# A transformer decoder layer and a non-local block in float32: reciprocal softmax sums turned on VectorE and spread by DMA instead of on TensorE, and the last perceptron block finished by row tile

## The chip, the cores and the metric

The kernel runs on one core of one Trainium2 chip. The metric is the device time of one execution in microseconds (us). Lower is better.

## What is computed

The reference takes `x` (16 x 256 x 512), a context of the same shape and two masks, all float32. It computes a decoder layer: layer norm, self-attention, layer norm, cross-attention on the context, layer norm, a perceptron of width 2048 with GELU, each with its residual. A non-local block of 1x1 convolutions follows. Cut to what matters here:

```python
def attention(q, k, v, mask):                    # 16 heads of 32 columns
    scores = jnp.einsum('bhqd,bhkd->bhqk', q, k) / jnp.sqrt(jnp.float32(HD))
    scores = scores * mask - 10000.0 * (1.0 - mask)
    probs = jax.nn.softmax(scores, axis=-1)
    return jnp.einsum('bhqk,bhkd->bhqd', probs, v)
...
x = hidden + attention(...) @ w_ao + b_ao        # then the same with the context
mlp_out = gelu(ln_out @ w1 + b1) @ w2 + b2
x = x + mlp_out
...
W = jnp.einsum('bnc,bcm->bnm', theta_x, phi_x) / phi_x.shape[-1]
y = jnp.einsum('bnm,bmc->bnc', W, g_x).transpose(0, 2, 1)
return bn(conv(w_w, w_b, y)) + x
```

## The kernel before

Every matrix product of weights and activations is made of three products of fp32r parts: each operand is split into a high part (ACT) and the rest (DVE), and `product` (L63 to L68) issues high x high, high x low and low x high.

The program has three stages. `step` (16 times) folds the non-local block's phi and g into one 128 x 256 matrix per batch and writes it to DRAM (`m1t`). Then come 16 attention blocks (8 of self-attention, 8 of cross-attention), each of two batches (512 tokens), in 17 bodies `body(r, k)` of 8 slots. Then come 8 perceptron blocks of 16 slots (`m_body`). Bodies 10 to 14 and perceptron blocks 1 to 6 are hardware loops.

A **group** is four heads of one batch; a block has 8 groups, 128 in all. A group goes through the slots of the attention stage as a pipeline, and every engine has its own in-order list of work per slot (`slot` of each engine). Around one group, in the slots that follow each other:

- Slot of its scores: PE `scores` (L850), near the end of a slot.
- Next slot: DVE `mask_scores` (L1361) and `maxima` (L1371). The slot after: ACT `exponential` (L1098), which writes exponentials `p` and row sums `rsum`.
- Slot "own": PE turns the four heads' exponentials (L867, four 128 x 128 transposes for each head, heads 0 and 1 at the slot's start, heads 2 and 3 in its middle). ACT copies them out of PSUM (L1104). DVE takes the reciprocals of the row sums (`inverses`, L1378, a 128 x 8 instruction). POOL copies each reciprocal 32 times side by side (`widen`, L657) into `rwide`. At the slot's end PE weighs the values (`weigh`, L880), unnormalised, into columns 0 to 255 of a PSUM bank, and turns `rwide` with two 128 x 128 transposes (L884) into columns 256 to 511 of the same bank, so that every one of the 32 columns of a head, now partitions, has its head's reciprocals along the tokens.
- Slot after it: ACT copies the turned reciprocals to SBUF (`sums_out`, L1112, tile `rt`), DVE multiplies (`scaled`, L1384), ACT and DVE split the product (`weighed`).

```python
                pe.wait_ge(wide_ok, grp + 1)
                for t in range(TPB):
                    last = pe.transpose(banks[:, bank, S + t * P:S + (t + 1) * P],
                                        rwide[:, t, :, :].rearrange("p j d -> p (j d)"), ident[:, :])
                last.then_inc(done, 1)
```

Between these, PE works on two units of 12 products per slot (q, k, v of the coming block, o of the block before). The o units end in DVE `unit_out` (L1340), which adds a residual tile `res` that SP has loaded (`load_res`, L456) and POOL has added a bias to (`add_bias`, L645); SP stores it (`store`, L460). `res` has two places, so tiles 2 and 3 are loaded when tiles 0 and 1 are stored. POOL also normalises the next block's rows (`normalise`, L640), which PE turns in slots 6 and 7 (`turn_rows`, L776); PE waits there for `ln_x`. POOL begins what it does in a slot only when DVE has the slot's maxima (`until_maxima`).

All DMAs are issued by SP, in order. Within a slot SP waits for whatever a transfer needs before it issues it and all that follow: stores for `y_ok` (late in the slot), loads of rows for `x_lo`, chunks of perceptron weights for the split of an earlier chunk.

At the end of each perceptron block, DVE adds the perceptron's PSUM result to the residual (L1587, four row tiles of 128 x 512, after one semaphore for all four), ACT and DVE split two row tiles at a time (`split_t`, L1246 and L1548, and the fold matrix, L1248 and L1550), PE makes theta (`theta`), ACT and DVE read it out (L1253, L1556), PE makes the last product (`last_product`), DVE adds (L1564), SP stores (L484). For all blocks but the last this lies inside the next block; for the last one it is the tail of the program (`after`), where the two batches' products share two PSUM banks and the two places of `res`.

## Time and profile before

| | |
|---|---|
| median of 3 runs | 2146.6 us (2146.05 to 2148.44) |
| time of the profiled execution | 2146.55 us |
| its span, first to last instruction | 2144.6 us |
| TensorE (PE) busy | 2111.4 us, 98% of the span |
| VectorE (DVE), ScalarE (ACT), GpSimd (POOL) busy | 65%, 56%, 22% |
| granted TensorE clock, mean | 0.996 of full speed |
| DMA | 126.24 MB, mean 59 GB/s |

"Busy" is the union of an engine's instructions in time, so overlapping ones count once. A mean duration of one matmul is longer than its distance to the next, since matmuls are pipelined. "Idle before, releaser" is the time an engine stood still before an instruction and who ended it. The chain is followed back from the last instruction, at each step to what released it.

### The profile page before, as it was taken

How to read it: one execution, taken by the hardware profiler on the slowest of the kernel's cores; microseconds unless marked ns; L12 is line 12 of the kernel's file. 1: busy time of each engine (PE TensorE's matmuls, PEld its weight loads, DVE VectorE, ACT ScalarE, POOL GpSimd, SP SyncE). 2: the span in 40 equal slices, each digit the busy share in tenths (PEclk: the TensorE clock that was granted, in tenths of full speed). 3: DMA queues.
4: the chain of work that ended last, by engine and by line, in shares of the span. 5: the costliest groups of instructions: out<-in, count | busy, mean ns of one | idle time of the engine just before them, and what ended most of it. 6: DMA issues, size and time to landing. Idle time of an engine off the chain costs nothing.

```text
span 2144.6 us, 42719 instructions
## 1 busy us (share of the span) xinstructions
PE 2111.4 (98%) x14690; PEld 1684.0 (79%) x14690; DVE 1396.8 (65%) x3693; ACT 1203.9 (56%) x3396; POOL 465.7 (22%) x515
## 2 busy tenths in 40 slices
PE   8989999999999999999999999999999999999998
PEld 7867777777777777777777776778888888888886
DVE  7687877777778877787877879565343343435333
ACT  4387878777888888787887878521111111111111
POOL 1012021111114233223223221043031230313000
PEclk9999999999999999999999999999999999999999
DMA  8410110110121231122122021321101011101001
GB/s 281 137 46 21 40 60 21 41 60 27 35 99 55 75 105 55 51 74 70 38 68 83 24 79 65 106 85 45 42 22 44 20 44 39 40 24 44 22 23 44
DMA packets 77273, 126.24 MB, mean 59 GB/s; under 512 B 7504, under 2 KB 25040, under 8 KB 77136
## 3 DMA queue, kind: packets, MB, share of 16 engines
q1 hardware_dynamic: 77136, 124.45, 17.4%
q8 instruction: 81, 1.33, 0.3%
q14 instruction: 56, 0.46, 0.1%
HBM read 97.16 MB, written 27.26 MB: 58 GB/s over the span
## 4 chain that ended last, share of the span: by engine, by line
PE 91%; DVE 2%; issue 1%; DMA 0%; ACT 0%; DVEq 0%; ACTq 0%
PE A_banks L66 11%; PE A_banks L68 11%; PE A_banks L67 11%; PE A_tp L867 10%; PE A_banks L880 6%; PE A_sc L66 6%; PE A_sc L68 6%; PE A_sc L67 6%; PE A_tp L67 5%; PE A_tp L66 5%; PE A_tp L68 5%; PE A_sc L850 5%; PE A_banks L884 2%; PE A_tp L776 1%; DVE A_p L1371 1%
## 5 line engine op out<-in xcount | busy, mean ns | idle before, releaser
L1098 ACT ACTIVATE A_p<-A_p,A_nmax 128x256 f32<-128x256 f32 x1024 | 510.7, 510 | 0.0
L1361 DVE TENSOR_TENSOR A_p<-A_sc,A_mk 128x1024 f32<-128x1024 f32 x256 | 312.3, 1220 | 203.8 <-PE A_tp L867 203.8
L1104 ACT ACTIVATE A_pt<-A_tp 128x512 f32<-128x512 f32 x512 | 278.6, 596 | 235.9 <-PE A_tp L867 235.9
L1371 DVE CUSTOM_DVE_ANT_0 A_p<-A_p,A_ma 128x256 f32<-128x256 f32 x1024 | 381.1, 427 | 5.5
L867 PE MATMUL A_tp<-A_ident,A_p 128*128 128x128 f32 x2048 | 266.0, 273 | 1.4 <-ACT A_pt L1104 1.4
L867 PEld LDWEIGHTS A_tp<-A_ident,A_p 128*128 128x128 f32 x2048 | 235.0, 141 | 20.1 <-issue 2.4
L1098 ACT ACTIVATION_READ_ACCUMULATOR A_p<-A_p,A_nmax 128x1 f32 x1024 | 205.4, 201 | 0.0
L657 POOL COPY A_rwide<-A_rinv 128x256 f32<-128x256 f32 x128 | 51.4, 401 | 693.2 <-DVE A_ct_l L1391 693.2
L1231 ACT ACTIVATE A_mk<-A_tp,A_cols 128x512 f32<-128x512 f32 x62 | 42.7, 689 | 276.8 <-PE A_tp L68 276.8
L1231 ACT ACTIVATE A_ma<-A_tp,A_cols 128x512 f32<-128x512 f32 x62 | 42.7, 688 | 247.9 <-PE A_tp L68 247.9
L66 PE MATMUL A_banks<-A_xt_h,A_w_h 128*128 128x512 f32 x384 | 161.9, 421 | 0.0
L68 PE MATMUL A_banks<-A_xt_h,A_w_l 128*128 128x512 f32 x384 | 152.1, 396 | 0.0
L67 PE MATMUL A_banks<-A_xt_l,A_w_h 128*128 128x512 f32 x384 | 151.4, 394 | 0.0
L66 PE MATMUL A_tp<-A_xt_h,A_w_h 128*128 128x512 f32 x368 | 145.7, 396 | 0.0
L67 PE MATMUL A_tp<-A_xt_l,A_w_h 128*128 128x512 f32 x368 | 145.6, 396 | 0.0
L68 PE MATMUL A_tp<-A_xt_h,A_w_l 128*128 128x512 f32 x368 | 145.5, 395 | 0.0
L1533 DVE CAST A_h_h<-A_ma 128x512 fp32r<-128x512 f32 x64 | 31.5, 492 | 172.8 <-ACT A_ma L1231 169.0
L880 PE MATMUL A_banks<-A_pt,A_v 128*32 128x256 f32 x2048 | 139.0, 389 | 0.0
L1533 DVE CAST A_h_h<-A_mk 128x512 fp32r<-128x512 f32 x64 | 35.2, 549 | 158.9 <-ACT A_mk L1231 156.2
L744 POOL TENSOR_TENSOR A_v<-A_v,A_b_row 128x512 f32<-128x512 f32 x32 | 53.7, 1700 | 381.0 <-DMA A_v<-x 381.0
L66 PE MATMUL A_banks<-A_w_h,A_ct_h 128*128 128x512 f32 x256 | 107.5, 420 | 0.0
L67 PE MATMUL A_banks<-A_w_l,A_ct_h 128*128 128x512 f32 x256 | 100.9, 394 | 0.0
(223 smaller groups left out, 5032.3 us busy)
## 6 DMA issues: line engine op xcount, KB each, us to landing
A_x<-x SPq DMA_DIRECT2D x96, 256.0 KB, 3.7
A_res<-x SPq DMA_DIRECT2D x64, 256.0 KB, 2.7
x<-A_res SPq DMA_DIRECT2D x64, 256.0 KB, 2.3
A_e<-ctx SPq DMA_DIRECT2D x16, 512.0 KB, 4.2
A_e<-ctx_t SPq DMA_DIRECT2D x16, 512.0 KB, 6.5
A_e<-L_xattn_w SPq DMA_DIRECT2D x32, 256.0 KB, 3.1
A_v<-x SPq DMA_DIRECT2D x32, 256.0 KB, 2.8
out<-A_res SPq DMA_DIRECT2D x32, 256.0 KB, 2.0
```

What stands on the lines that cost most here:

```text
L66: pe.matmul(out, sh, mh, start=first, stop=False)
L67: pe.matmul(out, sh, ml, start=False, stop=False)
L68: return pe.matmul(out, sl, mh, start=False, stop=last)
L850: last = pe.matmul(sc[:, j, t * S:(t + 1) * S], qp[rr, f, rows_], kp[rr, f, keys], start=(n == 0), stop=(n == 2))
L867: last = pe.transpose(tp[:, j % 2, c * S + t * P:c * S + (t + 1) * P], p[:, g % 2, j, t, c * P:(c + 1) * P], ident[:, :])
L880: pe.matmul(banks[rr, bank, 0:S], v[:, b * TPB + c, f * P + j * HD:f * P + (j + 1) * HD], pt[:, j, c, :], start=(c == 0), stop=(c == TPB - 1))
L1098: act.activation(p[:, g % 2, j, t, :], p[:, g % 2, j, t, :], ACT.Exp, scale=-1.0, bias=nmax[:, g % 2, j, t:t + 1], accum_out=rsum[:, g % 2 ...
L1104: act.activation(pt[:, j, :, :], tp[:, j % 2, :].rearrange("p (c s) -> p c s", c=TPB), ACT.Copy)\
L1231: act.activation(hf[f % 4], hidden_bank(blk, f), ACT.Gelu_apprx_tanh, bias=b1_col[:, f:f + 1])\
L1361: dve.tensor_tensor(p[:, g % 2, heads, :, :].rearrange("p j t s -> p j (t s)"), sc[:, heads, :], m, ALU.mult)\
L1371: dve.tensor_tensor_reduce(out=a_, in0=a_, in1=ma[:, b, t, :], scale=-1.0, scalar=BIG, op0=ALU.add, op1=ALU.min, accum_out=nmax[:, g % 2, ...
L1533: dve.tensor_copy(h_h[:, f % 2, :], hf[f % 4]).then_inc(h_hi, 1)
```

## The change

**Reciprocals.** `rinv` becomes 128 x 32 per parity (zeroed once), of which DVE writes 8 columns (one for each pair of row tile and head). A second DVE instruction turns each 32 x 32 block of it: the four blocks' first 8 rows then hold the reciprocals along the tokens. SP writes these four pieces (8 partitions x 128 B each) to a small DRAM tensor `inverses`, waits for them to land, and reads them back with four DMAs, one for each head, each spread over that head's 32 partitions (32 x 2 x 512 B), straight into `rt`. DVE's `scaled` waits for the weighing and for that landing. `widen`, the two transposes of `weigh` and `sums_out` are gone. SP does this first in each slot with an own group, and the two later `load_res` are moved: tiles 0 and 1 from slot 7 to slot 0 of the next body, tiles 2 and 3 from slot 5 to slot 6.

**End of the perceptron.** For the last block alone, the fold matrices are split one slot before the end (with tiles of their own), PE's last `second` signals each row tile, DVE, ACT and DVE again work by single row tiles, the last products of batch 0 go to the two `tp` banks, and the outputs of batch 1 to two tiles of `x`.

The rest: one early fold of four biases is moved by one slot, `w_s` lives in `rt`, and `b2_row` gets smaller.

```diff
+            def store_inverses(r, h):
+
+                grp, _, g = group(r, h, -1)
+                wait_apart(sp, inv_t, grp + 1, ld_i, (grp - 1) * HPG * DMA)
+                for n in range(P // 32):
+                    sp.dma_start(inv_dram[g % 2][:, n * 32:(n + 1) * 32], turned_inv[n * 32:n * 32 + TPB * HPG, g % 2, :])\
+                        .then_inc(st_i, DMA)
+
+            def load_inverses(r, h):
+
+                grp, _, g = group(r, h, -1)
+                wait_apart(sp, st_i, (grp + 1) * (P // 32) * DMA, cx_ok, grp)
+                for j in range(HPG):
+                    rr = slice(j * HD, (j + 1) * HD)
+                    own = inv_dram[g % 2].rearrange("(t j) s -> j t s", j=HPG)[j:j + 1]
+                    sp.dma_start(rt[rr, :].rearrange("p (t s) -> p t s", t=TPB), own.broadcast_to([HD, TPB, P]))\
+                        .then_inc(ld_i, DMA)
...
             def slot(r, k, h, a_, b_, own, pv):
+                if own:
+                    store_inverses(r, h)
+                    load_inverses(r, h)
+                if h == 0 and k > 1:
+                    for t in range(2):
+                        load_res(k - 1, r - 1, t)
+                if h == (6 if k < NU else 4) and k:
+                    for t in range(2):
+                        load_res(k - 1, r - 1, t + 2)
...
                 if h == (5 if k < NU else 3) and k:
                     for t in range(2):
                         store(k - 1, r - 1, t)
-                        load_res(k - 1, r - 1, t + 2)
...
                             store(k - 1, r - 1, t + 2)
-                            if k < NU:
-                                load_res(k, r, t)
...
-                if own:
-                    widen(r, k, h)
...
-                pe.wait_ge(wide_ok, grp + 1)
-                for t in range(TPB):
-                    last = pe.transpose(banks[:, bank, S + t * P:S + (t + 1) * P],
-                                        rwide[:, t, :, :].rearrange("p j d -> p (j d)"), ident[:, :])
                 last.then_inc(done, 1)
...
-                if leaves:
-                    sums_out(r, h, pv)
...
             def inverses(r, h):
                 grp, _, g = group(r, h, -1)
                 dve.wait_ge(exped, (grp + 1) * HPG * TPB)
-                dve.reciprocal(rinv[:, g % 2, :, :], rsum[:, g % 2, :, :]).then_inc(inv_ok, 1)
+                dve.reciprocal(rinv[:, g % 2, 0:TPB * HPG], rsum[:, g % 2, :, :].rearrange("p t j -> p (t j)"))\
+                    .then_inc(inv_ok, 1)
+                wait_apart(dve, inv_ok, grp + 1, st_i, (grp - 1) * (P // 32) * DMA)
+                dve.transpose(turned_inv[:, g % 2, :], rinv[:, g % 2, :]).then_inc(inv_t, 1)
 
             def scaled(r, h, pv):
                 grp, _, g = group(r, h, -2)
-                dve.wait_ge(rt_ok, grp + 1)
+                dve.wait_ge(done, pv[1])
+                dve.wait_ge(ld_i, (grp + 1) * HPG * DMA)
                 wait(dve, c_lo, grp)
...
             def after(items):
-                split_t(NB - 1, 0, True)
-                split_t(NB - 1, 1, True)
+                for t in range(TT):
+                    dve.wait_ge(a_end, t + 1)
+                    add_perceptron(NB - 1, t)
+                    if t == 2:
+                        split_end(0)
+                        split_end(1)
+                split_end(2)
+                split_end(3)
                 for item in items[:2]:
                     theta_out(item, NB, True)
                 for item in items[2:]:
-                    last_out(item, NB)
+                    last_out(item, NB, True)
```

How this moves instructions is shown at three places. First PE at the end of an attention slot (the weighing of a group, then the turns of the next), before:

```order
L850 MATMUL A_sc<-A_k_l,A_q_h 128x256 x4
L850 MATMUL A_sc<-A_k_h,A_q_l 128x256 x4
L880 MATMUL A_banks<-A_pt,A_v 32x256 x8
L884 MATMUL A_banks<-A_ident,A_rwide 128x128 x2
L867 MATMUL A_tp<-A_ident,A_p 128x128 x8
L66 MATMUL A_banks<-A_xt_h,A_w_h 128x512
```

and now:

```order
L876 MATMUL A_sc<-A_k_l,A_q_h 128x256 x4
L876 MATMUL A_sc<-A_k_h,A_q_l 128x256 x4
L906 MATMUL A_banks<-A_pt,A_v 32x256 x8
L893 MATMUL A_tp<-A_ident,A_p 128x128 x8
L66 MATMUL A_banks<-A_xt_h,A_w_h 128x512
```

The two transposes between the weighing and the next turns are gone; nothing else of PE's attention slots has moved.

Second SP's queue in slots 5 to 7 and slot 0 of an attention body, with what each row waits for (`A_y_ok`: DVE's output tile; `A_st_y0`, `A_st_y1`: the store that frees a place of `res`; `A_inv_t`: the turned reciprocals; `A_st_i`: their stores; `A_cx_ok`: the multiply that frees `rt`), before:

```order
L460 DMA x<-A_res 128x512 [waits A_y_ok]
L456 DMA A_res<-x 128x512 [waits A_st_y0]
L460 DMA x<-A_res 128x512 [waits A_y_ok]
L456 DMA A_res<-x 128x512 [waits A_st_y1]
L460 DMA x<-A_res 128x512 [waits A_y_ok]
L456 DMA A_res<-x 128x512 [waits A_st_y0]
L460 DMA x<-A_res 128x512 [waits A_y_ok]
L456 DMA A_res<-x 128x512 [waits A_st_y1]
L441 DMA A_x<-x 128x512 [waits A_x_lo] x4
```

and now, from the stores of slot 5 to those of slot 7:

```order
L471 DMA x<-A_res 128x512 [waits A_y_ok] x2
L502 DMA inverses<-A_turned_inv 8x32 [waits A_ld_i,A_inv_t]
L502 DMA inverses<-A_turned_inv 8x32 x3
L512 DMA A_rt<-inverses 32x2x128 [waits A_cx_ok,A_st_i]
L512 DMA A_rt<-inverses 32x2x128 x3
L467 DMA A_res<-x 128x512 [waits A_st_y0]
L467 DMA A_res<-x 128x512 [waits A_st_y1]
L502 DMA inverses<-A_turned_inv 8x32 [waits A_ld_i,A_inv_t]
L502 DMA inverses<-A_turned_inv 8x32 x3
L512 DMA A_rt<-inverses 32x2x128 [waits A_cx_ok,A_st_i]
L512 DMA A_rt<-inverses 32x2x128 x3
L471 DMA x<-A_res 128x512 [waits A_y_ok] x2
```

The load of residual tiles 2 and 3 stood right behind the stores of tiles 0 and 1; now four stores, a wait for their landing, and four loads stand ahead of it.

Third DVE at the end of the program, before:

```order
L1587 TENSOR_TENSOR A_v<-A_sc,A_v 128x512 x4
L1548 TENSOR_TENSOR A_t_l<-A_v,A_t_h 128x1024
L1550 TENSOR_TENSOR A_m_l<-A_m,A_m_h 128x256
L1548 TENSOR_TENSOR A_xt_l<-A_v,A_xt_h 128x1024
L1550 TENSOR_TENSOR A_xt_l<-A_x,A_xt_h 128x256
L1556 SCALAR_TENSOR_TENSOR A_thx_l<-A_banks,A_cols,A_thx_h 128x512
L1556 SCALAR_TENSOR_TENSOR A_xt_l<-A_banks,A_cols,A_xt_h 128x512
L1564 SCALAR_TENSOR_TENSOR A_res<-A_banks,A_fix,A_v 128x512 x4
```

and now:

```order
L1603 TENSOR_TENSOR A_v<-A_sc,A_v 128x512 x3
L1598 TENSOR_TENSOR A_t_l<-A_v,A_t_h 128x512 x2
L1603 TENSOR_TENSOR A_v<-A_sc,A_v 128x512
L1598 TENSOR_TENSOR A_xt_l<-A_v,A_xt_h 128x512 x2
L1609 SCALAR_TENSOR_TENSOR A_thx_l<-A_banks,A_cols,A_thx_h 128x512
L1609 SCALAR_TENSOR_TENSOR A_xt_l<-A_banks,A_cols,A_xt_h 128x512
L1618 SCALAR_TENSOR_TENSOR A_res<-A_tp,A_fix,A_v 128x512 x2
L1618 SCALAR_TENSOR_TENSOR A_x<-A_banks,A_fix,A_v 128x512 x2
```

The splits of the fold matrices have left the tail, and the splits of the result go by row tile, two of them ahead of the last add.

## Rows read from the trace of the kernel before

**Rows 1.** The page, busy time, share of the span, instructions: TensorE matmuls

```profile
PE 2111.4 (98%) x14690; PEld 1684.0 (79%) x14690; DVE 1396.8 (65%) x3693; ACT 1203.9 (56%) x3396; POOL 465.7 (22%) x515
```

**Rows 2.** Busy time by stretch: PE, PEld, DVE, ACT, POOL, PEclk, DMA share, GB/s

```profile
300.00:700.00 400.00, 400.00 (x3412) 313.68 (x3405) 315.83 (x978) 322.82 (x982) 78.21 (x104) 1.00 0.16 51
...
2100.00:2145.00 45.00, 34.85 (x142) 26.96 (x140) 16.87 (x24) 6.75 (x10) 2.99 (x2) 0.93 0.15 53
```

**Rows 3.** Waits: engine line, waited for, us in total, times, longest us

```profile
ACT A_pt L1104 <- PE A_tp L867: 235.9, 251, 3.6
DVE A_p L1361 <- PE A_tp L867: 203.8, 122, 3.1
```

**Rows 4.** Timeline of PE where a slot ends: start us, us, engine, line

```profile
603.79 1.07 PE L880 MATMUL A_banks<-A_pt,A_v 128*32 128x256 f32 x16
604.79 0.44 PE L884 MATMUL A_banks<-A_ident,A_rwide 128*128 128x128 f32 x2
605.07 1.04 PE L867 MATMUL A_tp<-A_ident,A_p 128*128 128x128 f32 x8
```

**Rows 5.** Groups of PE: busy us, mean ns of one, idle before

```profile
L884 PE MATMUL A_banks<-A_ident,A_rwide 128*128 128x128 f32 x256 | 56.2, 301 | 0.0
```

**Rows 6.** Instructions on tile rt: duration ns min/median/max, first and last start

```profile
L1112 ACT ACTIVATE A_rt<-A_banks x128: 379/391/396, 126.4 to 1366.8; 128x256 f32<-128x256 f32 x128
```

**Rows 7.** Timeline of DVE, slots 5 and 6 of an attention body

```profile
587.29 0.19 DVE L1378 RECIPROCAL A_rinv<-A_rsum 128x8 f32<-128x8 f32 x1
...
596.90 0.19 DVE L1378 RECIPROCAL A_rinv<-A_rsum 128x8 f32<-128x8 f32 x1
597.01 0.37 DVE L1384 TENSOR_TENSOR A_cx<-A_banks,A_rt 128x256 f32<-128x256 f32 x1
```

**Rows 8.** DMA issues: KB each, median us from issue to landing

```profile
A_x<-x SPq DMA_DIRECT2D x96, 256.0 KB, 3.7
A_res<-x SPq DMA_DIRECT2D x64, 256.0 KB, 2.7
x<-A_res SPq DMA_DIRECT2D x64, 256.0 KB, 2.3
...
out<-A_res SPq DMA_DIRECT2D x32, 256.0 KB, 2.0
```

**Rows 9.** Timeline of SP's queue: time from first to last issue

```profile
617.31 1.85 SPq L441 DMA_DIRECT2D A_x<-x  x4
```

**Rows 10.** Timeline of POOL in slot 6, and of PE in slot 7

```profile
602.05 2.56 POOL L645 TENSOR_TENSOR A_res<-A_res,A_o_bias 128x512 f32<-128x512 f32 x2 [2.33 <-DVE A_nmax L1371]
604.57 1.54 POOL L640 TENSOR_SCALAR A_x<-A_x,A_nmean,A_rstd 128x512 f32<-128x512 f32 x2
...
611.00 1.03 PE L776 MATMUL A_tp<-A_ident,A_x 128*128 128x128 f32 x8
```

**Rows 11.** Timeline of the end of the program

```profile
2126.33 0.39 PE L67 MATMUL A_sc<-A_w_l,A_h_h 128*128 128x512 f32 x1
2126.56 0.39 PE L68 MATMUL A_sc<-A_w_h,A_h_l 128*128 128x512 f32 x1
2126.98 2.48 DVE L1587 TENSOR_TENSOR A_v<-A_sc,A_v 128x512 f32<-128x512 f32 x4 [3.59 <-PE A_sc L68]
2128.30 1.06 ACT L1246 ACTIVATE A_t_h<-A_v 128x1024 fp32r<-128x1024 f32 x1 [6.10 <-DVE A_v L1587]
...
2129.39 1.23 DVE L1548 TENSOR_TENSOR A_t_l<-A_v,A_t_h 128x1024 fp32r<-128x1024 f32 x1
...
2130.72 0.47 PE L66 MATMUL A_banks<-A_t_h,A_thw_h 128*128 128x512 f32 x1 [3.78 <-issue]
...
2132.52 0.69 ACT L1253 ACTIVATE A_thx_h<-A_banks,A_cols 128x512 fp32r<-128x512 f32 x1 [1.60 <-PE A_banks L68]
2132.76 0.63 PE L67 MATMUL A_banks<-A_xt_l,A_thw_h 128*128 128x512 f32 x1
...
2140.58 0.75 DVE L1564 SCALAR_TENSOR_TENSOR A_res<-A_banks,A_fix,A_v 128x512 f32<-128x512 f32 x1 [0.43 <-DMA out<-A_res]
```

More of the change, by code:

```diff
@@ L288, in operands, with unit_bank, y_tile @@
                 return (whole, x[:, 0, 0:S], (xt_h[:, 0:TPB, :], xt_l[:, 0:TPB, :]),
-                        (xt_h[:, TPB, 0:S], xt_l[:, TPB, 0:S]), (xt_h[:, TPB + 1, :], xt_l[:, TPB + 1, :]))
+                        (m1_end_h[:, :], m1_end_l[:, :]), (xt_h[:, TPB, :], xt_l[:, TPB, :]))
             return whole, m1[:, :], (t_h[:, :, :], t_l[:, :, :]), (m1_h[:, :], m1_l[:, 0:S]), (thx_h[:, :], thx_l[:, :])
+        def unit_bank(item, end=False):
+            (kind, n, _), (bank, _) = item
+            return tp[:, n[1], :] if end and kind == "p" and n[0] == 0 else banks[:, bank, :]
+        def y_tile(b, o, end=False):
+            return x[:, TPB + o, :] if end and b == BPB - 1 else y[:, o, :]
         def hidden_bank(blk, f):
@@ L993, in hidden, with second @@
                 last.then_inc(h_done, 1)
-            def second(blk, f, first):
+            def second(blk, f, first, end=False):
                 if first:
@@ L1007, in second @@
                                    (hi, lo), f == 0, f == FT - 1)
-                last.then_inc(a_done, 1)
+                    if end:
+                        last.then_inc(a_end, 1)
+                if not end:
+                    last.then_inc(a_done, 1)
             def theta(item, blk, end=False):
@@ L1012, in theta @@
                 m_occupy((kind, b, rel), bank, blk)
-                pe.wait_ge(t_lo, (blk + rel) * BPB + (b + 1))
+                if not end:
+                    pe.wait_ge(t_lo, (blk + rel) * BPB + (b + 1))
                 pe.wait_ge(m1_lo, 1)
@@ L1016, in theta @@
                 for t in range(TPB):
+                    if end:
+                        pe.wait_ge(t_lo, B - BPB + b * TPB + t + 1)
                     cols_ = slice(t * CI, (t + 1) * CI)
@@ L1025, in last_product @@
                 tb = blk + unit[2]
-                m_occupy(unit, bank, blk)
+                if not (end and b == 0):
+                    m_occupy(unit, bank, blk)
                 pe.wait_ge(m1_lo, tb * BPB + (b + 2))
@@ L1030, in last_product @@
                 cols_ = slice(o * P, (o + 1) * P)
-                product(pe, banks[:, bank, :], (mh[:, cols_], ml[:, cols_]), thx, True, True).then_inc(m_done, 1)
+                product(pe, unit_bank(item, end), (mh[:, cols_], ml[:, cols_]), thx, True, True).then_inc(m_done, 1)
             def m_slot(blk, f, first, last, unit, turns):
@@ L1045, in m_slot @@
                         m_turn(item, blk, False)
-                    second(blk, f, first)
+                    second(blk, f, first, last)
             def after(items):
@@ L1105, in turned_out @@
                     .then_inc(pt_ok, 1)
-            def sums_out(r, h, pv):
-                grp, _, g = group(r, h, -2)
-                bank, count = pv
-                act.wait_ge(done, count)
-                wait(act, cx_ok, grp)
-                act.activation(rt[:, :], banks[:, bank, S:2 * S], ACT.Copy).then_inc(rt_ok, 1)
             def weighed(r, k, h):
@@ L1265, in m_slot @@
                     m_turned(item, blk)
+                if last and f == FT - 2:
+                    split_fold(blk, 0, True)
+                    split_fold(blk, 1, True)
             def after(items):
-                split_t(NB - 1, 0, True)
-                split_t(NB - 1, 1, True)
+                for t in range(TT):
+                    split_end(t)
                 for item in items[:2]:
@@ L1562, in last_out @@
                 dve.wait_ge(m_done, count)
-                dve.wait_ge(st_y[o], (NU * 2 + tb * BPB + b) * DMA)
-                dve.scalar_tensor_tensor(y[:, o, :], banks[:, bank, :], fix[:, o:o + 1], t_sb[:, b * TPB + o, :],
+                if not (end and b == BPB - 1):
+                    dve.wait_ge(st_y[o], (NU * 2 + tb * BPB + b) * DMA)
+                dve.scalar_tensor_tensor(y_tile(b, o, end), unit_bank(item, end), fix[:, o:o + 1], t_sb[:, b * TPB + o, :],
                                          ALU.add, ALU.add).then_inc(y_ok, 1)
@@ L1581, in m_slot @@
                     m_turned(item, blk)
-                if f == FT - 1:
+                if last and f == FT - 2:
+                    split_fold(blk, 0, True)
+                    split_fold(blk, 1, True)
+                if f == FT - 1 and not last:
                     n = blk * FT + f
@@ L1585, in m_slot @@
                     for t in range(TT):
[L1586 to L1587 removed]
+                        add_perceptron(blk, t)
             def after(items):
[L1590 to L1591 removed]
+                for t in range(TT):
+                    dve.wait_ge(a_end, t + 1)
[5 more added lines that the diff above has]
+                split_end(3)
                 for item in items[:2]:
```

96 lines of the change are left out of this document (55 added, 41 removed).

## The prediction

> **What bounds the kernel now.** I began with the page's line of busy times [rows 1]: TensorE is busy 98% of the span, VectorE 65%, ScalarE 56%. Busy time alone doesn't say that TensorE is the limit, so I went to the stretches. From 300 to 700 us, inside the attention stage, TensorE shows 400.00 busy us of 400 at full granted clock (1.00, the 2.4 GHz level), with VectorE at 79% and ScalarE at 81% [rows 2]. Then the waits, to see who waits for whom. ScalarE waits 235.9 us for TensorE's turns in 251 places, VectorE 203.8 us in 122 [rows 3]. Over 128 groups that is 1.8 and 1.6 us per slot in which the two stand idle for TensorE. So the attention stage runs at TensorE's pace, and an instruction taken off TensorE there shortens a slot, as long as nothing else needs more than those 1.6 us. The tail is different: in the last 45 us TensorE is busy for 34.85 only, at a mean granted clock of 0.93 [rows 2]. There a chain of adds, splits, products and stores sets the end.
>
> **The turns on TensorE, removed.** There are 256 in 128 pairs, 56.2 us busy, 301 ns each [rows 5]. The distance between starts is what counts. In the timeline a pair starts at 604.79 and the next group's turns at 605.07, 0.28 us later. Those eight turns of the same shape take 1.04 us in all [rows 4]. If the last lasts about as long as the mean of such a turn (301 ns is the nearest row), their seven distances are (1.04 - 0.30) / 7 = 0.106 us each. The first two starts after the weighing are further apart (0.28 for two steps, so about 0.17 and 0.11). That extra belongs to the step from the weighing's shape to a turn's and will stand in front of the next turns instead. So a pair is worth 2 x 0.11 = 0.22 us, and the sum 128 x 0.22 = 28 us. The upper end is 128 x 0.28 = 36 us, if the extra goes too. The lower end is 14 us, if half is given back because the waits that the next turns stand behind (exponentials done, copies out done) are now taken up one after the other where the pair used to cover them. I take 28: the same kind of waits stand before the other turns of a slot.
>
> The Trainium skill ("TensorE: Matmul & The Clock Gate", Part 4: PE-mode transpose) gives a turn about 275 ns in a kernel's context. By that the sum would be an estimated 256 x 0.275 = 70 us. The timeline speaks against it, since the whole pair takes 0.28 us of TensorE's time.
>
> **ScalarE, VectorE and GpSimd in a slot.** ScalarE loses its copy, 391 ns [rows 6]. It waits for TensorE anyway, so that is worth nothing, and it is a reserve. GpSimd loses the widening; it is no bound at 22% [rows 1]. VectorE gains a turn of 128 x 32 and a wait for its own reciprocal. No row shows a turn on VectorE. The nearest are the reciprocal, 0.19 us, and the multiply of 128 x 256, 0.37 us [rows 7]. I take 0.2 for the turn and 0.1 for the wait, since the multiply now starts 0.11 us after the reciprocal's start, overlapped, and the turn cannot. That 0.3 us (ends 0.2 and 0.5) lies within the 1.6 us of idle time. If that cover were gone, it would cost up to 128 x 0.3 = 38 us. Only at the end of the attention stage, where perceptron weights are split as well, do I expect it to show in two or three slots, under 1 us, about what ScalarE's 0.39 gives back there.
>
> **The way through DRAM.** This is the new long wait. From the turned reciprocals to the multiply of the next slot go four stores, their landing, four loads and their landing. An issue costs SP about 1.85 / 4 = 0.46 us, loads of 256 KB back to back [rows 9]. These are smaller, and I keep the price. A store lands 2.3 us after its issue, a load of `res` 2.7 [rows 8]; the new ones are of 1 KB and of 32 KB each, so the times should be no longer while the queue is empty. Round trip: 0.3 + 3 x 0.46 + 2.3 + 3 x 0.46 + 2.7 = 8.1 us. What is there for it: reciprocals start 9.61 us apart (587.29 and 596.90), and the multiply follows its slot's reciprocal by 0.11 [rows 7]. Less the 0.19 of the reciprocal and the 0.22 that the slot gets shorter, that leaves 9.3 us, and VectorE's 1.6 idle us come on top, 10.9 in all. So 8.1 fits, with 1.2 us to spare before anything waits and 2.8 before TensorE does. The last of `done` comes at the slot's end, so nothing is gained on the other side. The load is also held back by `rt`'s single place, but the multiply that frees it comes right behind the reciprocal, long before the stores land.
>
> **SP's queue.** Its eight new issues are 3.7 us per slot, and SP stands about 6 us in a slot's first half. Behind it: in slot 0 two `res` loads and four row loads (2.8 us), with contexts and a mask in the later bodies. They are wanted a slot or more later, so I cost them at nothing. The burst of slot 0 is also ahead of slot 1's small transfers in the DMA queue. Row loads land in 3.7 us [rows 8], one us over the 2.7 taken, which still fits. The tight one is `res` in slot 6. Reciprocal end 597.09 plus 0.3, stores out and landed at +3.7 (601.1), loads issued until 602.9, the first `res` load landed at 605.6, the second half a microsecond later. GpSimd's two adds (2.56) and two normalisations (1.54) [rows 10] used to begin at 602.05. From 605.6 they end at 609.7. TensorE turns those rows at 611.00 [rows 10], 0.2 earlier in the new slot. 1.1 us are left. I cost it at nothing; it is rival B.
>
> **The tail.** Before: last products start 2126.56, one each 0.23 us [rows 11]. Four adds take 2.48 us (0.62 each), and the first waits for all tiles. The chain then goes by halves of 128 x 1024 (ACT 1.06, DVE 1.23) to the first theta product at 2130.72, on to theta's read-out, and to the last add at 2140.58. From there theta's products run at 0.43 us or more apart for a while (the row at 2132.76 lasts 0.63, not 0.39), which is the clock's lower level after 3.78 us without products.
> Now: tile 0's last product is done 9 x 0.23 = 2.1 us before tile 3's, so adds run at 2124.9, 2125.6 and 2126.3. ScalarE's half-size copies (0.6) follow each. DVE splits tiles 0 and 1 from 2127.0 to 2128.3, adds tile 3 until 2128.9, splits tiles 2 and 3 until 2130.2. Theta of batch 0 can start 2127.7, 3.0 us earlier. That of batch 1 ends at 2131.1; read-out 0.7 and 0.75 gives 2132.6. The products of batch 0 don't wait for the other theta's bank, the outputs of batch 1 don't wait for stores. Four final adds back to back from 2132.6, 0.7 each, end at 2135.4, where the last one ended at 2141.3. That is 5.9 us at full clock. Six to twelve products may run at half clock, up to 12 x 0.2 = 2.4 us back, and four stores within 2.8 us may land later than the usual 2.0 [rows 8]. I take 5 us, ends 3 and 6.
>
> **Sum.** 2146.55 (the profiled execution, within 0.1 us of the median 2146.6, so it stands for it) - 28 - 5 = 2113.5 us. The memset, the moved bias fold and the smaller row cost nothing beside TensorE's 100%.
>
> **Rivals.**
> A, half the gain on TensorE: 14 + 5 = 19 us, 2127.6. For it: no row shows the waits of the turns without the pair in front. Against: TensorE shows no gap anywhere between 300 and 700 us. Chance 0.10.
> B, late `res` in slot 6: the normalised rows are late for the turns of slot 7 in 15 bodies. It decides when the chain above is over 1.1 us longer. At transfers landing in 3.7 instead of 2.3 and 2.7 it is 1.4 + 1.0 + 1.0 = 3.4 us longer: 15 x 2.3 = 34 us back, 2147.5, no change; at half of that lateness, 15 x 0.6 = 9 us, 2122.5. Chance 0.12, half of it for each.
> C, the round trip is longer than 10.9 us and sets the slot: slower. At 3.7 us landing for both and 0.46 an issue it is 0.3 + 1.4 + 3.7 + 1.4 + 3.7 = 10.5, just inside. At one us more, since a store must have landed in DRAM before its read may go, it is 11.5: 0.6 over in some 124 slots, 74 us, or 2146.6 - 33 + 74 = 2188. For it: nothing in the trace shows a write that is read back at once, nor pieces of 128 B. Chance 0.07. The Trainium skill ("DMA: Bandwidth & Descriptors", Specifications) says that transfers under 512 B are made by read-modify-write, which these stores are; no run here shows its price.
> D, each turn gives back all its 301 ns: 77 + 5 = 82 us, 2064.5. This is what the skill's rule above amounts to. Chance 0.01.
> The forecast has 0.70. That the change doesn't do what it says is out: in the order of instructions the pair is gone.
>
> **Numbers.** The forecast's own range is 2104.5 (36 and 6 us) to 2123. With A inside and part of B, the range for 8 in 10 is 2103 to 2133. A measurement of this kernel can tell about 0.2%, 4.3 us, from no change. Faster by more than that: the forecast, A, D and the milder half of B, 0.70 + 0.10 + 0.01 + 0.06 = 0.87. Within: the other half of B, 0.06. Slower: C, 0.07.
>
> **What would show it.** Right: distance from the weighing's start to the next turns about 1.06 us instead of 1.28; reciprocals 9.4 us apart in slots like [rows 7]; TensorE still 100% busy in the attention stage; from issue to landing of the small transfers at most 2.7 us; the first theta product 1.1 us after the perceptron's last product starts, not 4.2; the end of the last add 8.9 us after that start, not 14.8. Wrong: a wait of DVE's multiply for the load of `rt` with more than a few us in all (C); TensorE's turn of rows waiting for GpSimd's normalisation (B); a longer "issue" gap in front of the turns (A).

## The result, and the profile after

The changed kernel took 2137.9 us (median of 6 runs, 2132.3 to 2140.8), the kernel before 2147.2 in the same comparison (6 runs, 2146.1 to 2148.4): a ratio of 0.9954, 95% interval 0.9939 to 0.9969. It is faster by 9.3 us, where 33 were forecast; the forecast of 2113.5 us and its range of 2103 to 2133 both miss. Its runs also lie 8.5 us apart, those of before 2.4. The profiled execution took 2140.8 us with a span of 2138.9, so what is read below is one of the slower ones: 5.7 us less than the span before.

The page's busy times and the stretches, with the columns of [rows 1, 2]:

```profile
PE 2092.2 (98%) x14434; PEld 1657.3 (77%) x14434; DVE 1433.6 (67%) x3823; ACT 1171.5 (55%) x3270; POOL 419.1 (20%) x388
```
```profile
300.00:700.00 400.00, 395.26 (x3334) 306.62 (x3327) 331.58 (x1022) 313.49 (x945) 65.48 (x63) 1.00 0.20 64
700.00:1000.00 300.00, 293.18 (x2501) 225.77 (x2500) 245.56 (x759) 233.41 (x705) 77.86 (x70) 1.00 0.26 81
1000.00:1300.00 300.00, 296.24 (x2492) 229.46 (x2492) 247.75 (x768) 232.99 (x707) 67.88 (x64) 1.00 0.23 75
```

TensorE is no longer busy throughout the attention stage: it stands idle 4.7, 6.8 and 3.8 us in these stretches. The end of an ordinary slot, answering to [rows 4]:

```profile
597.36 1.07 PE L906 MATMUL A_banks<-A_pt,A_v 128*32 128x256 f32 x16
598.37 0.87 PE L893 MATMUL A_tp<-A_ident,A_p 128*128 128x128 f32 x6
```

From the weighing's start to the next turns it is 1.01 us, where it was 1.28. The saving is there in every ordinary slot. From one weighing's start to the next (the same row in each slot) it was 9.61 us, 10.48 where rows are turned too; now 9.40 and 10.27. So 0.21 us per slot are saved, where 0.22 were forecast. Yet the last weighing starts at 1365.28 us, against 1365.37 before. What the ordinary slots gain, others give back. The intervals by slot, in us, computed from those starts:

```
body       slot 2   slot 3   slot 7   (bodies 2 to 5: 9.39, 9.41, 10.29)
7          11.17    10.05    14.94
8          11.65    10.57    10.29
9          10.89    10.95    10.29
10         10.19    10.05    10.54
11         9.39     9.92     10.29
12         10.02    10.07    10.29
13         9.39     9.94     10.29
14         9.59     10.05    10.29
15         11.62    10.05    9.44
```

Slot 7 of body 15 has no rows to turn. Over bodies 7 to 15 slot 2 is 9.4 us too long in all, slot 3 7.0, and slot 7 of body 7 4.7. Now the waits (engine line, waited for, us in total, times, longest us), first of VectorE, then of TensorE:

```profile
DVE A_cx L1422 <- DMA A_rt<-inverses: 18.5, 9, 3.4
```
```profile
PE A_banks L66 <- DVE A_cx L1422: 6.3, 5, 2.0
PE A_banks L66 <- DVE A_k_l L1379: 5.1, 10, 1.3
PE A_tp L802 <- POOL A_x L675: 2.8, 2, 2.1
```

The multiply waits 18.5 us for `rt`'s load, in nine slots: one in each of bodies 7 to 15, in slot 2, for the transfers of slot 1. TensorE waits behind it for its bank, and a slot later for k's read-out, which the late multiply pushed back. Below is SP's queue (start, time from first to last issue), first an ordinary slot of body 6, then body 10 from the inverses of slot 0 to the loads of slot 1, and VectorE's rows at the end of the latter:

```profile
562.81 1.28 SPq L502 DMA_DIRECT2D inverses<-A_turned_inv  x4
565.04 1.73 SPq L512 DMA_DIRECT2D A_rt<-inverses  x4
...
856.82 1.32 SPq L502 DMA_DIRECT2D inverses<-A_turned_inv  x4
859.08 1.73 SPq L512 DMA_DIRECT2D A_rt<-inverses  x4
861.11 1.70 SPq L467 DMA_DIRECT2D A_res<-x  x2
863.11 2.11 SPq L452 DMA_DIRECT2D A_x<-x  x4
865.56 1.10 SPq L458 DMA_DIRECT2D A_e<-ctx_t  x2
866.96 0.37 SPq L463 DMA_DIRECT2D A_mk<-mask_Bx1xSxS_ff  x1
867.54 2.07 SPq L502 DMA_DIRECT2D inverses<-A_turned_inv  x4
874.40 1.73 SPq L512 DMA_DIRECT2D A_rt<-inverses  x4
```
```profile
865.93 0.21 DVE L1415 STREAM_TRANSPOSE A_turned_inv<-A_rinv 128x32 f32<-128x32 f32 x1
...
875.06 0.20 DVE L1412 RECIPROCAL A_rinv<-A_rsum 128x8 f32<-128x8 f32 x1
875.34 0.21 DVE L1415 STREAM_TRANSPOSE A_turned_inv<-A_rinv 128x32 f32<-128x32 f32 x1
877.60 0.42 DVE L1422 TENSOR_TENSOR A_cx<-A_banks,A_rt 128x256 f32<-128x256 f32 x1 [2.04 <-DMA A_rt<-inverses]
```

In an ordinary slot the stores are issued right after the turn and the loads 0.95 us after the last store was issued (564.09 to 565.04): SP waits for the stores' landing there, so stores of 1 KB take no longer than that. From the turn's end to the landing of the loads it is about 5.5 us. In body 10 the turn of slot 1 ends at 866.14, but SP is still issuing slot 0's loads until 867.33. Then the four stores stand behind 2.75 MB of slot 0's loads. The loads can only be issued 4.8 us after the last store (869.61 to 874.40), and the multiply starts 11.5 us after the turn's end, having waited 2.04. The longer the delay, the longer the slot: where the multiply starts 10.50 and 10.54 us after the turn's end (bodies 11 and 13), slot 2 loses nothing, at 10.85 (body 14) 0.2, at 11.28 (body 12) 0.6, at 11.46 (body 10) 0.8, at 12.3 (body 7) 1.8. Body 9 alone falls out of this row: 10.65 and 1.5 lost, and there TensorE waits 1.34 us for VectorE's masking.

The 14.9 us of body 7, slot 7, have another chain. Rows of SP, POOL and PE there:

```profile
670.14 0.43 SPq L447 DMA_DIRECT2D A_wst<-L_xattn_w_q  x1
674.05 0.33 SPq L447 DMA_DIRECT2D A_wst<-L_xattn_w_kv  x1
674.49 1.31 SPq L502 DMA_DIRECT2D inverses<-A_turned_inv  x4
677.33 2.42 SPq L512 DMA_DIRECT2D A_rt<-inverses  x4
679.79 0.90 SPq L467 DMA_DIRECT2D A_res<-x  x2
```
```profile
672.57 1.46 POOL L705 TENSOR_TENSOR A_w_l<-A_wst,A_w_h 128x512 fp32r<-128x512 f32 x1
682.86 2.76 POOL L680 TENSOR_TENSOR A_res<-A_res,A_o_bias 128x512 f32<-128x512 f32 x2 [8.83 <-DVE A_nmax L1405]
685.60 2.20 POOL L675 TENSOR_SCALAR A_x<-A_x,A_nmean,A_rstd 128x512 f32<-128x512 f32 x2
```
```profile
686.51 0.63 PE L802 MATMUL A_tp<-A_ident,A_x 128*128 128x128 f32 x4 [2.08 <-POOL A_x L675]
687.86 1.11 PE L802 MATMUL A_tp<-A_ident,A_x 128*128 128x128 f32 x4 [0.72 <-POOL A_x L675]
```
```profile
684.00:688.00 4.00, 1.20 (x7) 0.56 (x6) 4.00 (x10) 1.26 (x5) 4.00 (x5) 0.95 0.28 98
688.00:691.00 3.00, 3.00 (x10) 2.42 (x10) 1.38 (x4) 1.99 (x8) 2.92 (x3) 0.50 0.00 0
```

SP stands in `load_chunk` until GpSimd has split the chunk before (674.03). Slot 6's inverses and the `res` loads behind them go out 4 us late, then GpSimd's add and its normalisation, and TensorE's turn of rows waits, 2.8 us in all. The slot is 4.7 us too long, not 2.8, in part because TensorE, busy for 1.20 of 4 us, then runs 3 us at a granted clock of 0.50 (the 1.2 GHz level; the last two rows are stretches with the columns of [rows 2]).

The tail, answering to [rows 11]:

```profile
2126.78 0.39 PE L68 MATMUL A_sc<-A_w_h,A_h_l 128*128 128x512 f32 x1
2127.96 0.47 PE L66 MATMUL A_banks<-A_t_h,A_thw_h 128*128 128x512 f32 x1 [0.80 <-DVE A_t_l L1598]
```
```profile
2134.16 1.40 DVE L1618 SCALAR_TENSOR_TENSOR A_x<-A_banks,A_fix,A_v 128x512 f32<-128x512 f32 x2
```
```profile
2095.00:2138.90 43.90, 38.51 (x164) 30.00 (x162) 16.98 (x28) 7.88 (x13) 2.98 (x2) 0.99 0.15 55
```

The first theta product starts 1.18 us after the perceptron's last product, the last add ends (2135.56) 8.8 us after it; 1.1 and 8.9 were forecast. From the last weighing to the end of the span it was 779.2 us and is 773.6. The granted clock of the last 44 us is 0.99, where it was 0.93 in the last 45 [rows 2].

### The profile page after: what moved, and what is told of

Same layout as the page of the kernel before. It is cut to its first block and busy times, and to the rows that moved or that the text cites. A ratio compares the mean times of both kernels' runs of the same rounds, so it can differ in the third digit from the quotient of the medians.

```text
span 2138.9 us, 43342 instructions
## 1 busy us (share of the span) xinstructions
PE 2092.2 (98%) x14434; PEld 1657.3 (77%) x14434; DVE 1433.6 (67%) x3823; ACT 1171.5 (55%) x3270; POOL 419.1 (20%) x388
## 5 line engine op out<-in xcount | busy, mean ns | idle before, releaser
L1405 DVE CUSTOM_DVE_ANT_0 A_p<-A_p,A_ma 128x256 f32<-128x256 f32 x1024 | 387.5, 435 | 6.1 <-DVE A_p L1395 0.5
L893 PEld LDWEIGHTS A_tp<-A_ident,A_p 128*128 128x128 f32 x2048 | 229.9, 141 | 73.3 <-issue 51.0
L893 PE MATMUL A_tp<-A_ident,A_p 128*128 128x128 f32 x2048 | 274.2, 277 | 1.7 <-ACT A_pt L1133 1.4
L680 POOL TENSOR_TENSOR A_res<-A_res,A_o_bias 128x512 f32<-128x512 f32 x64 | 82.5, 1310 | 353.3 <-DVE A_nmax L1405 208.3
L1140 ACT ACTIVATE A_ct_h<-A_cx,A_bias_sum 128x256 fp32r<-128x256 f32 x128 | 65.2, 510 | 88.0 <-DVE A_cx L1422 88.0
```

Of the source, the lines that this page charges most:

```text
L680: pool.tensor_tensor(res[:, t % 2, :], res[:, t % 2, :], o_bias[:, int(k >= NB), :], ALU.add)\
L893: last = pe.transpose(tp[:, j % 2, c * S + t * P:c * S + (t + 1) * P], p[:, g % 2, j, t, c * P:(c + 1) * P], ident[:, :])
L1405: dve.tensor_tensor_reduce(out=a_, in0=a_, in1=ma[:, b, t, :], scale=-1.0, scalar=BIG, op0=ALU.add, op1=ALU.min, accum_out=nmax[:, g % 2, ...
```

## Experiments

Three explanations of the missing time are tried. T1 says that slot 0's loads hold up slot 1's round trip. R1 says that GpSimd's work, moved by the later `res` loads, stretches VectorE's maxima, and R2 that VectorE's added turn and wait cost the time. For R1 there is a row: one of the maxima of 128 x 256 takes 1.16 us beside GpSimd's add, where the others take 0.41:

```profile
601.50 1.16 DVE L1405 CUSTOM_DVE_ANT_0 A_p<-A_p,A_ma 128x256 f32<-128x256 f32 x1
...
602.59 0.41 DVE L1405 CUSTOM_DVE_ANT_0 A_p<-A_p,A_ma 128x256 f32<-128x256 f32 x1
```

**1. The tail alone.** The kernel before, with the change of the perceptron's end and nothing of the attention stage's.

> Before with the change's tail alone (perceptron by row tile, own banks and tiles for the last outputs); the reciprocal sums go over TensorE as before. From the last weighing to the end of the span the changed kernel needs 773.6 us, the kernel before 779.2. All theories: 2147.2 - 5.6 = 2141.5 us. Were the tail's gain due to the attention stage's change, it would stay at 2147.

Measured: 2141.2 us against 2148.2, ratio 0.9971 (0.9960 to 0.9982). The tail's 5 us are real: 7.0 by the medians, 6.5 between the profiled spans. So the whole change in the attention stage, some 28 us by the forecast, brought about 3, and even these are not clear of the noise, since the intervals of this run and of the change overlap.

**2. No round trip.** Left out: the way through DRAM, so VectorE multiplies by numbers that are not the reciprocals.

```
-                if own:
-                    store_inverses(r, h)
-                    load_inverses(r, h)
...
-                dve.wait_ge(ld_i, (grp + 1) * HPG * DMA)
```

> The changed kernel with the eight small transfers per head group left out (turned reciprocals stay where they are, VectorE multiplies by whatever the tile rt holds); VectorE's turn, the moved loads of res and GpSimd's moved work stay. T1 (the gain is given back because the loads of slot 0, issued by SP ahead of slot 1's small transfers, hold up the round trip): all but a few us of the 26 that are missing come back, 2112 to 2116 us. R1 (GpSimd's work, moved by the later res loads, runs beside VectorE's maxima and stretches them) or R2 (VectorE's added turn and wait): the missing time stays, 2132 to 2138 us. T1 in the intervals between weighings: slots 2 and 3 of bodies 7 to 15 at 9.4 us instead of 10 to 11.6.

Measured: 2119.7 us, 0.9871 (0.9856 to 0.9886, against before). 18 us come back; slots 2 and 3 of bodies 7 to 15 are at 9.4, but for 9.86 in body 9's slot 2, and slot 7 of body 7 at 10.29. VectorE's turn is still in this kernel, so R2 can't be the bulk. R1 is not tried by it, against what the expectation says: without the round trip SP issues the `res` loads earlier, GpSimd's work with them, and the maxima are busy for 380.9 us, as in the kernel before (381.1), and not the 387.5 of the change. Runs 3 and 7 bear on R1. The time is 4 to 8 us above the 2112 to 2116 of T1, so something is lost elsewhere too (run 10 finds a part).

**3. The burst spread.** One mask, the contexts and body 7's and 8's chunks leave slot 0.

```
                 if h == 0:
                     if k < NU:
                         load_rows(k + 1, r + 1)
-                    if NB <= k + 1 < NU:
-                        load_context(r + 1)
-                    if NB < k < NU:
-                        load_mask(r, 0)
-                    for n in {7: range(0, 4), 8: range(10, 12)}.get(k, ()):
-                        load_chunk(n)
...
+                if h == 1 and NB < k < NU:
+                    load_mask(r, 0)
+                if h in (1, 2) and NB <= k + 1 < NU:
+                    load_context(r + 1, h - 1)
+                if h == 1:
+                    for n in {7: range(0, 4), 8: range(10, 12)}.get(k, ()):
+                        load_chunk(n)
```

GpSimd's addend of that mask goes from slot 0 to slot 1, behind its two adds.

> The changed kernel with slot 0's burst shortened: context loads behind the inverses of slots 1 and 2, mask and weight chunks behind those of slot 1; res and row loads stay in slot 0. T1: bodies 7 to 15 look like bodies 2 to 6 in slots 2 and 3 (9.4 us each), which gives back 2.4 + 3.4 + 3.0 + 1.5 + 0.5 + 1.3 + 0.5 + 0.8 + 2.9 = 16 us by their intervals between weighings: 2121 to 2124 us; the 14.9 us interval of body 7, slot 7, stays. R1, R2: 2136 to 2140 us.

Measured: 2125.8 us, 0.9897 (0.9882 to 0.9912), 12 us less than the change, with the same number of transfers and the same turn on VectorE. All slots 2 and 3 of bodies 7 to 14 take 9.4 us; body 15, whose perceptron chunks and norm rows are still in slot 0, keeps 11.66 and 9.86. The view of tile rt shows what is left of the wait (what it waited for, us, times):

```profile
  DMA A_rt<-inverses: 4.3, 2
```

The wait was 18.5 us in nine slots and is 4.3 in two. The maxima are still stretched (385.7 us), so R1 can't be the bulk either. Run 2 kept the mask's addend in its place and had the short slots too, so the addend's move is not what shortens them: T1 stands. 2 us of the forecast are missing; body 8's slot 0 takes 11.0 us here.

**4. And body 7's chunks a slot apart.** `(7, 5): range(4, 6), (7, 6): range(6, 8)` in place of four chunks in slot 5.

> As the run before, and body 7's weight chunks 6 and 7 are loaded in slot 6 instead of 5, so that SP does not wait in slot 5 for GpSimd's split. If SP's wait for that split is what makes the 14.9 us interval in slot 7 of body 7 (inverse stores 3.9 us late, res loads behind them, then GpSimd's add and normalisation, then TensorE's turn of rows), another 4 to 5 us: 2116 to 2120 us. If that interval comes from the splits' own work on three engines, no difference to the run before.

Measured: 2122.6 us, 0.9885 (0.9870 to 0.9900). Slot 7 of body 7 is back at 10.29 from 14.49. The saving between the medians is 3.2 us where 4 to 5 were forecast, the time is above the expected 2116 to 2120, and the intervals of the two runs overlap; the profile shows the slot itself. The splits are all still there, so it was SP's wait.

**5. Slot 1's transfers on another queue.** ScalarE issues them; SP's burst stays.

```
                     turned_out(r, h, 1)
+                if own and h == 1:
+                    store_inverses(act, r, h)
...
                     weighed(r, k, h)
                 if own:
+                    if h == 1:
+                        load_inverses(act, r, h)
                     turned_out(r, h, 2)
```

> The changed kernel with the eight small transfers of slot 1, and only these, issued by ScalarE on its own DMA queue; slot 0's burst stays on SP, right ahead of them. Control inside the run: slot 2 in bodies 2 to 6, where no long burst stands ahead, shows what eight issues cost ScalarE (at SP's 0.45 us each 3.6 us against some 2.2 idle: intervals of about 10.8 instead of 9.4; if they are cheap for ScalarE, 9.4). Theory Q (the small transfers stand in one queue behind the burst): bodies 7 to 15 have the same slot 2 as bodies 2 to 6; 2122 to 2126 us if cheap, up to 2150 if 0.45 us each. Theory W (the sixteen DMA engines are simply busy with the burst, whichever queue a transfer is in): bodies 8, 9, 10 stay over 1 us longer than bodies 2 to 6; 2135 to 2140 us even if the issues are cheap.

Measured: 2230.1 us, 1.0381 (1.0367 to 1.0394), slower than any case foreseen. The timeline of ScalarE's queue in slot 1, body 3 and then body 10, says why:

```profile
324.92 1.32 ACTq L418 DMA_DIRECT2D inverses<-A_turned_inv  x4
...
327.36 1.76 ACTq L429 DMA_DIRECT2D A_rt<-inverses  x4
```
```profile
911.53 1.42 ACTq L418 DMA_DIRECT2D inverses<-A_turned_inv  x4
...
918.50 1.76 ACTq L429 DMA_DIRECT2D A_rt<-inverses  x4
920.37 1.09 ACT L1145 ACTIVATE A_pt<-A_tp 128x512 f32<-128x512 f32 x2 [5.46 <-issue]
```

The wait for the stores stands in ScalarE's own order: its next copy can't start before the loads are issued, and slot 1 takes 11.2 to 12.8 us in bodies 2 to 6 and 14.6 to 16.3 in bodies 7 to 15. My expectation had priced the issues (they take 0.33 and 0.44 us each, as on SP) and not this wait. It still tells queue and engines apart. In body 3 the loads follow the last store by 1.1 us, in body 10 by 5.5, with no other transfer in ScalarE's queue. So theory W holds: behind a burst a transfer is late in whichever queue it is. The Trainium skill ("DMA: Bandwidth & Descriptors", Issuing engines are not separate DMA queues) says that transfers from all issuing engines run on the same DMA engines; this trace agrees, with its 5.5 us. Only the part in which SP itself is late (1.4 us in body 10) could be gained by another issuer, and no run here shows that gain.

**6. One load for four heads.** The reciprocals stand by head, then row tile, so a head's 256 values are contiguous in DRAM.

```
+                own = inv_dram[g % 2].rearrange("(j t) s -> j (t s)", j=HPG).unsqueeze(1).to_broadcast([HPG, HD, S])
+                sp.dma_start(rt[:, :], own).then_inc(ld_i, DMA)
```

> The changed kernel with one load of 128 KB for the four heads instead of four of 32 KB (reciprocals kept by head, then row tile, so that a head's 256 values are contiguous). SP issues five transfers per slot instead of eight and the load's issue ends about 0.95 us earlier. T1: where slot 1's load lands late it lands 1 us less late, in slots 2 of bodies 7 to 12, 14, 15, and SP's own queue is shorter by the same in slot 0: 8 to 12 us, 2126 to 2130 us. If the stores and their wait behind the burst are all of it and the loads' issues lie elsewhere: 2135 to 2138 us.

Measured: 2127.6 us (2122.7 to 2131.7), 0.9911 (0.9898 to 0.9925), within T1's interval. The wait for `rt`'s load falls to 8.0 us in 6 slots. Three issues fewer per slot are worth 10 us, though not one of them is long. The load's issue takes 0.54 us instead of 1.73, so every round trip is 1.2 us shorter, and slot 0's burst is issued that much earlier: in body 10 slot 1's stores go out 0.1 us after the turn's end instead of 1.4, and the multiply waits 0.1 us instead of 2.04.

**7. The `res` loads in their old places.**

> The changed kernel with the four res loads of a body back in the places of the kernel before: right behind the stores of slots 5 and 7, so that SP waits there until a store has landed. R1 (the later res loads shift GpSimd's work onto VectorE's maxima, and that costs time): the shift is gone, 2130 to 2134 us. T1: SP is held up about 4 us at the start of slots 6 and 0; slot 6's round trip still fits (5.5 + 4 = 9.5 us), slot 0's burst is issued 4 us later and slot 1's inverses land later by up to as much: 1 to 4 us in each of bodies 7 to 15, 2147 to 2170 us.

Measured: 2136.3 us (2130.1 to 2148.8), 0.9954 (0.9937 to 0.9971), the same as the change. Both expectations miss. GpSimd's work is back in its place, and the maxima are busy for 380.3 us again instead of 387.5, at no gain to be seen. The run changes more than that, so it doesn't show by itself that R1 costs nothing: slot 7 of body 7 takes 10.65 us here instead of 14.94, while slot 2 of body 11 takes 13.47 instead of 9.39, and the multiplies wait 19.7 us for `rt` in 10 slots. But slot 7 of bodies 2 to 5, where the change has stretched maxima and this run has none, takes 10.29 us in both. My price for T1 was wrong as well, as SP's queue at body 10 shows:

```profile
853.77 0.33 SPq L467 DMA_DIRECT2D A_res<-x  x1
854.42 1.31 SPq L502 DMA_DIRECT2D inverses<-A_turned_inv  x4
857.18 3.24 SPq L512 DMA_DIRECT2D A_rt<-inverses  x4
860.73 2.18 SPq L452 DMA_DIRECT2D A_x<-x  x4
```

The burst starts later after slot 0's turn, but it has no `res` in it, 0.5 MB less; the multiply of slot 2 waits 2.17 us here, 2.04 in the change.

**8. The best version:** runs 3, 4 and 6 together, and the last body's first perceptron chunks in slots 1 and 2.

> Spread loads (contexts behind the inverses of slots 1 and 2, mask and chunks behind those of slot 1), body 7's chunks a slot apart, the last body's first four perceptron chunks in slots 1 and 2 instead of 0, and the one load of 128 KB. The run with the first two had 2122.6 us; body 15 still had 2.5 + 0.5 us too much in slots 2 and 3. T1: 2117 to 2120 us. Were body 15's excess not from its burst: 2121 to 2123 us.

Measured: 2120.7 us (2118.4 to 2121.5), 0.9875 (0.9861 to 0.9889), 0.7 us above T1's interval and 0.3 under the other case, so the time alone can't choose between them; body 15's slots can. It beats both kernels, the one before by 27 us. Body 15's slots 2 and 3 are at 9.39 and 9.41, and no multiply waits for `rt`'s load any more. SP's queue in slot 1 of body 10:

```profile
851.28 1.31 SPq L501 DMA_DIRECT2D inverses<-A_turned_inv  x4
853.53 0.54 SPq L509 DMA_DIRECT2D A_rt<-inverses  x1
854.41 0.42 SPq L462 DMA_DIRECT2D A_mk<-mask_Bx1xSxS_ff  x1
855.20 0.40 SPq L457 DMA_DIRECT2D A_e<-ctx_t  x1
```

**9. More burst where there was room.** Four loads of 256 KB into a free tile at the end of slot 0 in bodies 2 to 6.

> The changed kernel with four more loads of 256 KB (weights nobody reads, into a tile that is free then) at the end of slot 0's burst in bodies 2 to 6, whose slots 2 and 3 now take 9.4 us each and whose burst is 1.5 MB. With 2.5 MB they have about the burst of body 7 without its context. T1: their DVE multiply of slot 2 now waits for rt's load, 0.5 to 2 us each, and slot 3 is up to 0.6 us longer: 2140 to 2150 us. If the loss of bodies 7 to 15 comes from something else they do (mask addend, context split, chunk splits), bodies 2 to 6 stay at 9.4: 2137 to 2139 us.

Measured: 2139.9 us (2136.2 to 2144.8), 0.9965 (0.9953 to 0.9977): no difference that can be told from the change, and at the edge between the two cases foreseen. Only body 5 got longer (9.59 and 10.03 in slots 2 and 3), the others stayed at 9.4. Their loads did land later, 9.0 to 9.1 us after the turn's end instead of 6.0 to 8.0, but the multiply isn't wanted before 9.3; in body 5 it was 10.7 instead of 6.4. So 1 MB costs 1 to 4 us of landing and in four bodies of five nothing of time; the limit is sharp. T1 had the landing's direction right and left out the slack. In body 5:

```profile
465.50 1.80 SPq L602 DMA_DIRECT2D A_wst<-L_xattn_w_q  x4
467.41 1.71 SPq L503 DMA_DIRECT2D inverses<-A_turned_inv  x4
473.26 2.61 SPq L513 DMA_DIRECT2D A_rt<-inverses  x4
```

**10. No round trip and no turn.** Left out besides what run 2 leaves out: VectorE's turn of the reciprocals and its wait.

> As the run without the round trip (2119.7 us), and VectorE's turn of the reciprocals and its wait left out as well. There the attention stage saved 20.8 us between first and last weighing where 28 were forecast; bodies 1, 8, 9 and 16, in which VectorE also splits weights, fold biases or splits perceptron chunks, gave 0 to 1.4 us less than 1.66. If VectorE's extra 0.35 us per slot is what they miss: up to 4 bodies x 8 slots x 0.35 = 11 us, of which at most the missing 7 come: 2113 to 2117 us. If they are bound by something that neither has: 2118.5 to 2120.5 us.

Measured: 2116.8 us (2116.3 to 2117.6), 0.9858 (0.9843 to 0.9873), 2.9 less than run 2 by the medians; the intervals of the ratios overlap. The profiled last weighings are 2.3 us apart, 1.3 of it in the last body's five intervals (43.8 us, 45.1 in run 2) and 0.4 each in bodies 9 and 15; body 8 is the same. Body 1 takes 77.5 us for its eight slots (79.0 in run 2), but body 0 ends 1.4 us later here, so that is no gain. VectorE's turn and wait cost some 2 to 3 us, most of it in the last body.

**11. The bias fold back in slots 0 to 3** of the best version.

> The best version so far (spread loads and one load, 2120.7 us) with the fold of the last bias block in body 1 back in slots 0 to 3 instead of 1 to 4. Body 1's slots 0 and 2 take 10.8 and 10.15 us there. If slot 2's excess comes from the fold standing one slot later: back to about 9.6, and 2119.5 to 2120.5 us. If it is put where its weights (loaded in slot 0, now behind the inverses) are not there yet, VectorE waits in slot 0: 2121 to 2124 us.

Measured: 2124.0 us, 0.9895 (0.9879 to 0.9910), 3.3 more than run 8: the second case. VectorE waits 3.8 us once for the weights, which slot 0 now loads behind the inverses, and slot 1 of body 1 takes 12.5 us. So the moved fold belongs to the change.

## Why the prediction was wrong

**TensorE's turns, 28 us.** The price was right: 0.21 to 0.22 us per slot. The count was not. Without any round trip, the time from first weighing to last falls by 20.8 us, not 28 (run 2). An undisturbed body gives 1.7 us; bodies 0 and 1 give 0.4 together, body 8 0.3, bodies 9 and 15 1.1 each, and the last body's five intervals grow by 0.2. VectorE and ScalarE split weights in most of these; that this is why a shorter TensorE gives little there is argued, and run 10 shows a part of it. I had read 300 to 700 us and multiplied by all 128. Rival A had put the loss at 14 us, twice this one, and by another cause, waits in front of the turns.

**VectorE's turn.** 0.21 us, its start 0.28 after the reciprocal's: as put. That it would show "in two or three slots, under 1 us" was too low: 2 to 3 us by run 10.

**The round trip** was put at 8.1 us and takes 5.5 in an ordinary slot. The Trainium skill ("DMA: Bandwidth & Descriptors", Specifications) has transfers under 512 B made by read-modify-write, without a price; in this trace these stores, in pieces of 128 B, have landed 0.95 us after their issue.

**The step that failed** is the one on SP's queue: the loads of slot 0 "are wanted a slot or more later, so I cost them at nothing", and a landing of 3.7 us was "one us over the 2.7 taken, which still fits". I took the median landing of a row load for the delay of a transfer behind the whole burst. In bodies 7 to 15, with contexts, a mask or chunks in it, the loads of slot 1 were issued 7.3 to 9.5 us after the turn's end instead of 2.3 and landed after 10.5 to 12.7. That is over 9.3, at which the multiply is wanted, and in places over the 10.9 at which I had TensorE begin to wait, a limit that held (slot 2 lost nothing at 10.5 and 0.6 us at 11.3). A row of the kernel before had the number for a transfer behind the burst: the contexts, issued behind the row loads, landed after 6.5 us, the moving of their own 512 KB included.

```profile
A_e<-ctx_t SPq DMA_DIRECT2D x16, 512.0 KB, 6.5
```

With it for the landing of the stores, in place of 2.3, my own sum would have given 12.3 us, over the 10.9, in the bodies with a context (an estimate from that row). Between the change and run 2 the profiles' last weighings are 20.9 us apart: 19.6 in bodies 7 to 15, 3.6 up to the end of body 0, less 2.3 in the bodies left. By the medians the two kernels are 18.2 us apart; the change's profiled execution was one of its slower ones. It was rival C's mechanism, but in nine slots and not in 124.

**`res` in slot 6**, rival B: fitted in all bodies but one. In body 7 it failed by 4.7 us, because SP waited for GpSimd's split, which the prediction did not look at. The price of the rival was summed wrong as well: its 3.4 us counts the landing of `rt`'s loads (1.0), for which the `res` loads do not wait, so by its own terms it was 2.4 us longer, 1.3 late and 20 us in 15 bodies, not 34. And the 2123 us that closes the forecast's own range comes from none of the terms' ends.

**The tail.** 5 us forecast, 5.6 by the trace of the changed kernel, 7.0 in run 1 with an interval of about 2.4 us to either side. The sum at full clock was 5.9; of the up to 2.4 us for the lower clock little came, with 0.99 granted.

**What was said to show it:** the shorter step to the next turns came, TensorE's 100% did not, and a wait of the multiply for `rt` with "more than a few us in all" came, 18.5. Rival D is out: a turn's 301 ns were never TensorE's time between starts.

**Open:** the way from the start to the end of body 0 differs by up to 3.6 us between kernels with nearly the same code there (the first weighing at 121.9 us in run 8 and 123.7 in the change, the end of body 0 at 141.5 and 145.0). No run settles it, and it is as large as some of the differences above. Why body 8 gains only 0.3 us even in run 10 was not tried.

## What to carry to other kernels

A transfer that must be back within a slot was priced here not by its own size, nor by the queue it was in, but by the bytes issued in the slot before it: write down each slot's bytes ahead of it, body by body, and move what is wanted late behind it. Multiply a gain per slot only by the slots in which the engine that gains is the bound, and read that for every stretch of the program, not for one. Every transfer that was already in the kernel is a price for a new one behind the same burst: look for the row of the one issued last. And fewer transfers can be worth more than smaller ones: one load for four gave 10 us.

## What the runs showed of the hardware

A store of 1 KB in pieces of 128 B had landed 0.95 us after its issue with nothing ahead (the change, body 6), 4.8 us behind 2.75 MB (body 10), and 5.5 from a queue of its own beside such a burst (run 5). An issue costs SP 0.32 us for a store of 1 KB, 0.43 for a load of 32 KB with broadcast, 0.54 for one of 128 KB, 0.46 for the rows of 256 KB [rows 9], so the size hardly counts. TensorE, having stood idle for most of 4 us in body 7, ran the next 3 us at a granted clock of 0.50. VectorE turns 128 x 32 numbers in 0.21 us. One of its maxima took 1.16 us instead of 0.41 while GpSimd ran an add, and GpSimd's normalisations of two tiles took up to 2.63 us instead of 1.54 [rows 10].
